# A vision tower with product-key feed-forward on one core: front attention moved seven slots, search tiles one, gathered rows weighted on ScalarE, look-ups in fours, head masks as a two-tensor product

## What is computed

```python
h = tok(x); h = concatenate([cls_tok, h], axis=1)          # 64 x 65 x 64
# attention, 8 heads of 8 channels, cosine form
qn, kn = q / max(norm(q), 1e-12), k / max(norm(k), 1e-12)
attn = softmax(einsum(qn, kn) * scale + bias[None])
h = h + (einsum(attn, v)) @ proj_w.T + proj_b              # input layernormed
# feed-forward: per token and head the 16 best of 64 x 64 product keys
scores, idx = top_k(sim, 16)                               # two sides, 64 keys each
score = scores[0][..., :, None] + scores[1][..., None, :]
final_scores, pk_idx = top_k(score, 16); w = softmax(final_scores)
k = einsum(w, keys_table[ind]); v = einsum(w, values_table[ind])
h = h + softmax(causal(q @ k)) @ v @ Wo                    # input layernormed
```

## Time and profile before

| | us |
|---|---|
| median of 3 runs | 3051.8 (3051.78 to 3052.03) |
| the profiled execution: its own time | 3053.45 |
| its span, first to last instruction | 3051.4 |
| mean granted TensorE clock | 0.998 |
| units of pass 0 (5 images) | 258.7 |
| units of passes 1 to 6 (7 images), each | 309.4 to 310.7 |
| units of pass 7 (7 images, front of 5) | 300.4 |
| units of pass 8 and 9 (5 images) | 251.4 and 225.8 |

### The profile page before, as it was taken

How to read it: one execution, slowest core, us unless ns; L and a number is a source line. 1 busy time by engine, 2 the same in 40 slices (tenths; PEclk the granted TensorE clock), 3 DMA queues, 4 the chain that set the end, 5 groups by cost and what they waited for, 6 DMA issues and landing times.

```text
span 3051.4 us, 60054 instructions
## 1 busy us (share of the span) xinstructions
PE 2907.5 (95%) x16560; PEld 1968.0 (64%) x16560; DVE 2554.1 (84%) x10286; ACT 1730.3 (57%) x4926; POOL 1569.5 (51%) x3406
## 2 busy tenths in 40 slices
PE   8999999999999999999999999999999999999998
PEld 7867656665666566656665666566656666776666
DVE  4677789988998899889988898889888987777776
ACT  4465565555555555556555655565556555655554
POOL 2234356655665566555655565556655654333331
PEclk9999999999999999999999999999999999999999
DMA  9213211121111211121112111211121111010100
GB/s 214 50 45 79 52 31 33 32 37 34 32 32 31 41 29 32 32 40 30 30 31 45 25 32 32 40 31 33 32 38 33 33 33 38 20 24 20 25 20 19
DMA packets 121289, 117.47 MB, mean 38 GB/s; under 512 B 61491, under 2 KB 109310, under 8 KB 120958
## 3 DMA queue, kind: packets, MB, share of 16 engines
q1 hardware_dynamic: 105525, 83.84, 12.9%
q0 software_dynamic: 14336, 29.39, 5.6%
q10 hardware_dynamic: 1096, 0.41, 0.1%
HBM read 66.36 MB, written 9.84 MB: 25 GB/s over the span
## 4 chain that ended last, share of the span: by engine, by line
PE 53%; DVE 23%; issue 9%; POOL 7%; ACT 7%; ACTq 0%; DMA 0%; DVEq 0%; POOLq 0%
PE ps L831 27%; PE ps L819 11%; DVE wts L1230 11%; ACT wts L1005 4%; DVE x_sum L1297 2%; PE ps L755 2%; DVE top L1214 2%; PE ps L724 2%; PE ps L772 1%; PE ps L706 1%; POOL stat L528 1%; PE ps L862 1%; DVE cand_rest L1216 1%; DVE rest L1196 1%; POOL stat L525 1%
## 5 line engine op out<-in xcount | busy, mean ns | idle before, releaser
L831 PE MATMUL ps<-wts,table 128*128 128x455 f32 (+2 forms) x5120 | 2006.0, 474 | 0.0
L1230 DVE SCALAR_TENSOR_TENSOR wts<-ps,wts 128x455 f32<-128x455 f32 (+2 forms) x2560 | 1349.9, 531 | 383.4 <-ACT wts L1005 372.6
L819 PE MATMUL ps<-st,spread 128*128 128x456 f32 (+2 forms) x2560 | 1237.4, 483 | 119.0 <-DVE wts L1230 110.1
L1005 ACT ACTIVATE wts<-ps 128x455 f32<-128x455 f32 (+2 forms) x2560 | 1126.6, 475 | 86.8 <-PE ps L819 78.5
L831 PEld LDWEIGHTS ps<-wts,table 128*128 128x128 f32 x5120 | 905.4, 190 | 104.1 <-issue 44.4
L819 PEld LDWEIGHTS ps<-st,spread 128*128 128x128 f32 x2560 | 482.2, 188 | 603.0 <-DVE wts L1230 524.3
L591 POOL DMA_INDIRECT x_rows<-folded,x_r x448 | 453.8, 1013 | 85.9 <-issue 80.9
L524 POOL TENSOR_SCALAR stat<-top 110x1 f32<-110x1 f32 (+1 forms) x268 | 70.7, 264 | 760.1 <-DVE top L1214 756.2
L511 POOL TENSOR_TENSOR cand<-best 110x15 f32<-110x15 f32 (+5 forms) x804 | 160.4, 226 | 221.0 <-DVE best L1198 219.5
L980 ACT ACTIVATE cand_e<-top,stat 110x16 f32<-110x16 f32 (+1 forms) x268 | 82.3, 307 | 297.1 <-POOL stat L531 296.3
L976 ACT ACTIVATE sc<-ps 110x128 f32<-110x128 f32 (+1 forms) x268 | 74.2, 277 | 255.9 <-PE ps L772 255.6
(11 more groups left out here) (186 smaller groups left out, 3762.3 us busy)
## 6 DMA issues: line engine op xcount, KB each, us to landing
st<-st SPq DMA_DIRECT2D x320, 114.0 KB, 2.3
table<-in_table SPq DMA_DIRECT2D x128, 128.0 KB, 5.0
rz_row<-rz_dram SPq DMA_DIRECT2D x52, 165.0 KB
folded<-table SPq DMA_DIRECT2D x64, 128.0 KB, 2.6
x_rows<-folded,x_r POOLq DMA_INDIRECT x448
rz_row<-rz_dram SPq DMA_DIRECT2D x28, 228.0 KB
scratch<-in_x SPq DMA_DIRECT2D x7, 343.0 KB, 4.5
rz_dram<-rz SPq DMA_DIRECT2D x52, 1.3 KB
```

Of the source, the lines that this page charges most:

```text
L819: mm(ps[0:128, g % NA, 0:t], spread[:, q * 128:(q + 1) * 128], st[:, k % 2, ORDER[c // QUADS], 0:t], start=True, stop=True).then_inc(a_rea ...
L831: mm(ps[0:128, ACC + k % 2, 0:t], table[:, k % H, i, :], wts[:, g % RING, 0:t], start=(c == 0), stop=(c == CH - 1)).then_inc(out_done, 1)
L1005: A(wts[:, g % RING, 0:t], ps[0:128, g % NA, 0:t], ACT.Exp).then_inc(e_ready, 1)
L1230: V.scalar_tensor_tensor(out=wts[:, g % RING, 0:t], in0=ps[0:128, g % NA, 0:t], scalar=0.0, in1=wts[:, g % RING, 0:t], op0=ALU.is_ge, op1= ...
```

## The change

It alters six things:

1. `ATT` goes from `LN1` + 28 to `LN1` + 35. With that the task steps fall on slots 1 (mask), 3 (scores), 4, 5, 6 (POOL), 8, 11, 12, 14 of a head and the same plus 16; the reciprocal and the scaling move to task steps 12 and 13.
2. Tiles and picks start 15 slots ahead instead of 16 (`LEAD`).
3. The gathered blocks are multiplied by their weights on ScalarE, one instruction each (16 per pick, every third slot from 29), and VectorE adds blocks of four (three adds of 512 columns), then halves (256 and 128 columns).
4. The 16 look-ups are done four at a time: compare, multiply and reduce over 4 x 69 = 276 elements, 12 instructions in slots 17 to 28.
5. The sum of a task's exponentials comes from TensorE: the values get a column of ones (9 columns per head instead of 8), and the reciprocal reads PSUM. The VectorE sum (L1153) goes.
6. `kx` is made by a tensor-tensor product on POOL, and the layernorm's root and reciprocal become a power of -0.5 on POOL (slot +6); ScalarE only adds epsilon there. Some buffers move into `scratch`; the second buffers of `expo` (passes 1 to 9) and `pt` go.

```diff
-SLOTS = 4
+BATCH = 4
+BATCHES = TOPK // BATCH
+GAP = 3
+ADDS = 5
+GROUP = (0, 1, 2, 1)
-TILE_START = {CH * (k - 1) - 16 + 8 * (t + sparse(k)): (k, t) for k in range(HEADS) for t in range(tiles(k))}
-PICK_START = {CH * (k - 1) - 16: j for j, k in enumerate(PICKS)}
+LEAD = 15
+TILE_START = {CH * (k - 1) - LEAD + 8 * (t + sparse(k)): (k, t) for k in range(HEADS) for t in range(tiles(k))}
+PICK_START = {CH * (k - 1) - LEAD: j for j, k in enumerate(PICKS)}
-QK, VAL, NRM, ATT = LN1 + 11, LN1 + 14, LN1 + 17, LN1 + 28
+QK, VAL, NRM, ATT = LN1 + 11, LN1 + 14, LN1 + 17, LN1 + 35
-X_NEG, X_WEIGHT, X_POS, X_ZINV, X_NORM, X_ROW, X_FOUND = 13, 14, 15, 16, 17, 17, 21
-X_GATHER, X_ADD, X_TURN, X_MOVE = 22, 30, 77, 78
+X_NEG, X_WEIGHT, X_POS, X_ZINV, X_NORM, X_ROW, X_FOUND = 13, 14, 15, 16, 17, 17, 20
+X_GATHER, X_SCALE, X_ADD, X_TURN, X_MOVE = 22, 29, 39, 78, 79
...
 POOL, layernorm and mask
+            def layernorm(p, q, n, start):
+                i = 2 * p + n
+                if q == start + 6:
+                    pool.wait_ge(std_ready, i + 1)
+                    P.tensor_tensor(std[:, 0:PASSES[p]], std[:, 0:PASSES[p]], power[:, 0:PASSES[p]], ALU.pow)\
+                        .then_inc(inv_ready, 1)
-                    P.tensor_scalar(kx[0:C, 0:t], xf[:, 0:t], head_of[0:C, j:j + 1], None, ALU.mult)\
+                    P.tensor_tensor(kx[0:C, 0:t], xf[:, 0:t], head_of[0:C, j:j + 1].to_broadcast([C, t]), ALU.mult)\
...
 POOL, gathers
-                        if r % 4 == 0:
-                            pool.wait_ge(x_found, 4 * j + r // 4 + 1)
+                        if r % BATCH == 0:
+                            pool.wait_ge(x_found, BATCHES * (j + 1) if b == 2 else BATCHES * j + b + 1)
+                            if b == 0 and j >= 1:
+                                pool.wait_ge(x_turned, j)
+                            if b == 3:
+                                pool.wait_ge(x_add, ADDS * j + 1)
-                        if TOPK * j + r >= SLOTS:
-                            pool.wait_ge(x_add, TOPK * j + r - SLOTS + 1)
...
 ScalarE
-                    A(std[:, 0:PASSES[p]], ps[0:L, FR, 0:PASSES[p]], ACT.Sqrt, bias=eps[0:L, 0:1])\
+                    A(std[:, 0:PASSES[p]], ps[0:L, FR, 0:PASSES[p]], ACT.Identity, bias=eps[0:L, 0:1])\
+                for r in range(TOPK):
+                    j = pick_at(g, X_SCALE + GAP * r)
+                    if j is not None:
+                        if r == 0:
+                            act.wait_ge(x_norm, j + 1)
+                        act.wait_ge(x_in[r % (2 * BATCH)], 16 * (TOPK // (2 * BATCH) * j + r // (2 * BATCH) + 1))
+                        row = x_rows[:, GROUP[r // BATCH], r % BATCH, :]
+                        A(row, row, ACT.Copy, scale=x_w[:, j % 2, r:r + 1]).then_inc(x_scaled, 1)
...
 VectorE, attention of the front
-                j = task_at(p, q, 6)
-                if j is not None:
-                    dve.wait_ge(s_exp, base + j + 1)
-                    if j >= 2:
-                        dve.wait_ge(o_out, base + j - 1)
-                    V.tensor_reduce(red[:, j % 2, 1, 0:n], by_image(expo[:, j % 2, 0:t], n), AX.X, ALU.add)\
-                        .then_inc(s_sum, 1)
+                j = task_at(p, q, 12)
...
+                    V.reciprocal(red[:, j % 2, 1, 0:n], ps[0:L, bank("output", p), HD:n * (HD + 1):HD + 1])\
+                        .then_inc(s_inv, 1)
...
 VectorE, picks
+                for b in range(1, BATCHES):
+                    j = pick_at(g, X_ADD + GAP * BATCH * b)
+                    if j is not None:
+                        dve.wait_ge(x_scaled, TOPK * j + BATCH * (b + 1))
+                        if b >= 2:
+                            dve.wait_ge(x_add, ADDS * j + b - 1)
+                        V.tensor_tensor(x_rows[:, 0, :, :], x_rows[:, 0, :, :], x_rows[:, GROUP[b], :, :], ALU.add)\
+                            .then_inc(x_add, 1)
+                for half in (2, 1):
+                    j = pick_at(g, X_TURN - half)
...
-                        V.scalar_tensor_tensor(out=x_sum[:, :], in0=iota[:, :], scalar=x_pf[:, r:r + 1], in1=x_at[:, :],
-                                               op0=ALU.is_equal, op1=ALU.mult, accum_out=x_rf[:, r:r + 1])\
-                            .then_inc(x_row, 1)
+                        shape = [128, BATCH, NCAND]
+                        if step % 3 == 0:
+                            V.tensor_tensor(x_hit[:, :, :], iota[:, :].unsqueeze(1).to_broadcast(shape),
+                                            x_pf[:, BATCH * b:BATCH * (b + 1)].unsqueeze(2).to_broadcast(shape),
+                                            ALU.is_equal).then_inc(x_row, 1)
+                        if step % 3 == 1:
+                            V.tensor_tensor(x_hit[:, :, :], x_hit[:, :, :], x_at[:, :].unsqueeze(1).to_broadcast(shape),
+                                            ALU.mult).then_inc(x_row, 1)
+                        if step % 3 == 2:
+                            V.tensor_reduce(x_rf[:, BATCH * b:BATCH * (b + 1)], x_hit[:, :, :], AX.X, ALU.add)\
+                                .then_inc(x_row, 1)
```

## The result

The changed kernel takes 3144.4 us (3143.9 to 3146.5, four runs) against 3051.9 us: a ratio of 1.0304, 95% interval 1.0292 to 1.0316. It is slower by 93 us, where I forecast faster by 52. The time lies outside my range.

A forecast was written before the change was run, and what follows sets the result against it. TensorE was taken as the floor, with VectorE's lateness 7% above it. 3053.45 - 33 - 18 - 25 + 7 + 14 + 3 = 3001 us for the profiled execution, 3000 for the median; 8-in-10 range 2940 to 3054.

The forecast's parts named there:

- The three terms for the order of slots: Tiles one slot later -25 us, tasks piling up in slots 4 to 8 +14, second layernorm losing overlap in the prelude +3.
- The other terms: Less VectorE backlog -33 us, layernorms' table loads gone -18, the power late in POOL's slot 6 +7.
- The tiles one slot later: ScalarE's threshold wait moves from slots 14 and 30 to 15 and 31, 0.5 us off each place: -25 us (0 to 37).
- The pile-up of slots 4 to 8: Later tasks put 3.9 us on POOL before ScalarE's slot 8; charged 0.4 us in each of 36: 14 us (0 to 43).
- My third rival: POOL's 3.9 us chain in slots 4 to 8 isn't hidden and costs 115 us over 36 heads: 3101 us, chance 0.09.
- ScalarE's weightings: 448 added on ScalarE at 0.31 us, some 139 us against 51 us of table loads removed; taken as covered, no charge.
- VectorE's load: VectorE loses 434 us of work and gains 222, net 212 us; its busy time was to be near 2340 us.
- What that is worth: Lighter VectorE removes half of its own backlog's late spreads, 4.7 us in each of 7 passes: 33 us (0 to 66).
- (c): 38 late spreads of pass 3, 9.5 us together, put down to VectorE's own backlog.
- Table loads -18, power +7: Layernorms' two ScalarE loads per front go, 18 us; POOL's power at slot 6 delays TensorE, 0.4 us for each of 18.
- Head mask: POOL's tensor-tensor form was to cost 0.94 us instead of 1.45: 28 us less POOL time, no term in the sum.
- The rival about POOL: Look-ups in slots 6 to 9 stretched by POOL's run, 168 us of VectorE, backlog stays: 3033 us, chance 0.14.

The follow-up runs named there:

- the last run: Changed kernel with tasks, tiles, weighting, adding, look-ups and head mask as before, tile's sum one slot later on ScalarE: 0.9694, 2966.8 us against 3060.6, fastest of all.

## Why the prediction was wrong, point by point

The three terms for the order of slots (-25, +14 and +3 us) come to -8 us. They measured +79 us with the new instructions and +111 us in the kernel before. That is the step that failed most. The other terms (-33, -18 and +7 us) come to -44 us and measured +14 (1.0047).

*The tiles one slot later: -25 us, measured 0 alone, and some 40 us lost with the new forms.* The step that failed is "I take 0.5 us off each". The wait for the threshold comes from the distance of one slot between POOL's chain and ScalarE's sum, and both moved. Pass 9 of the changed kernel shows it as the prediction asked: slot 14 went from 0.85 to 0.10 us, but slot 31 keeps 0.79 of the 0.86 that slot 30 had, and slot 7 (0.55) and slot 28 (0.28) are new; the head has its 29.1 us as before. I had named this wait, and priced moving both ends of it. Moving one end, as the last run does with the tiles at their old slots, is worth 59 us (0.0194 of 3060).

*The pile-up of slots 4 to 8: +14 us charged, the largest cost.* Both moves together cost the kernel before 111 us, and putting the tasks alone back in the changed kernel gives 39 us. My third rival had the place and the engines (POOL's run from the threshold to the second subtraction, ScalarE at slot 8) and 3101 us, at 9 in 100. The chance was far too small, for two reasons that the rows could have told me. First, I counted POOL's work of slot 6 and left out slot 22, where a gather of 1.07 us stands between the chain and the subtraction; slots 23 and 24 hold 7.2 us of pass 3. (The sign that I had named, ScalarE idle for over 2 us at slot 8, didn't show in that form: there it waits some 0.3 us for the subtraction, after 1.6 us at the median for the threshold at slot 7, and 1.5 us at most at slot 24.) Second, "ScalarE and TensorE have other work there" was no argument against: the other work of ScalarE stood *behind* the waiting instruction.

*ScalarE's weightings: nothing charged, 28 us.* "Under its 40% of slack" is the failed step. The duration was also taken too low (0.31 us, where 0.39 were measured). The idle time of an in-order engine covers only what doesn't stand ahead of a unit that the chain of spreads waits for.

*VectorE's load: near 2340 us expected, 2437 measured.* The new instructions cost nearly what I had worked out, 233 us against 222 (the groups by form, compare):

```profile
L1323 DVE TENSOR_TENSOR x_rows<-x_rows 128x512 f32<-128x512 f32 x84 | 59.0, 702 | 0.0
L1346 DVE TENSOR_TENSOR x_rows<-iota,x_pf 128x276 f32<-128x276 f32 x112 | 58.1, 519 | 0.0
L1350 DVE TENSOR_TENSOR x_rows<-x_rows,x_at 128x276 f32<-128x276 f32 x112 | 49.1, 438 | 0.0
L1353 DVE TENSOR_REDUCE x_rf<-x_rows 128x4 f32<-128x276 f32 x112 | 47.4, 423 | 0.0
L1330 DVE TENSOR_TENSOR x_rows<-x_rows 128x256 f32<-128x256 f32 x28 | 11.6, 413 | 0.0
L1330 DVE TENSOR_TENSOR x_rows<-x_rows 128x128 f32<-128x128 f32 x28 | 7.6, 272 | 0.0
```

The error is in what the removed ones gave back. By the timeline a VectorE instruction starts before the one ahead of it has ended, so durations overlap: over the whole run they sum to 3190.9 us before and to 2991.5 after, while busy time is 2554.1 and 2437.1. Of 199 us of durations only 117 are time; 968 instructions fewer have each given back 0.085 us less than their row says.

*What that is worth: 33 us.* The column of ones alone gave 26. Batches and adds by fours removed instructions too and gained nothing: the second put its work on ScalarE, and with the first ScalarE waits longer. So (c) was not mainly VectorE's load; the fastest kernel has VectorE at 84%, as before, and half the lateness.

*Table loads -18, power +7: -11 us together, measured -8 ± 6.* Right in sum, wrong in the parts: the power takes 1.52 us for 7 columns, just above my upper bound and not in the lower third, and TensorE waits 1.64 us for it in the pass above. The layernorms' table loads went, and with them the exponential's reloads (59 to 21, where I had 20).

*Head mask: 28 us of POOL for nothing.* Hidden, I said; the two-tensor form costs 14 us (0.45%), by a way that I hadn't in mind, the 14 look-ups that it holds up. The rival about POOL, that it holds the new VectorE instructions, decided little: of the 112 first instructions of a batch 34 were stretched, by 9.8 us in all, not 168.

## To carry to other kernels

When each engine takes its instructions in a fixed order, look for instructions that wait for another engine with critical work queued behind them, and try moving the waiting end later, not the work. Here one slot on ScalarE was worth 59 us in one kernel, more than any saved work, and 14 us in another where the slot behind was taken, so it has to be measured in place. A change of places has to be priced together with the other changes of places: 0.7% and 0.0% made 3.6%. Slack of an engine is no cover for an instruction that stands ahead of the critical one.

## What the hardware showed that I had not expected

A power of -0.5 on POOL took 1.52 us for 65 x 7 elements, as long as a product with a scalar over 65 times as many columns. ScalarE's copy with a scale per partition took 0.39 us for 128 x 128 out of SBUF. POOL's tensor-tensor over 64 x 455 elements held 14 VectorE look-ups, which have two SBUF inputs, until its own end (1.74 instead of 0.27 us), and the product with a scalar in its place only slowed 14 of them (0.28 to 0.43 us), so that 0.96 us on POOL can cost more than 1.46. Small tensor-tensors of POOL, 110 x 15 to 110 x 32 elements, left a look-up beside them at 0.28 us. The Trainium skill (SBUF — State Buffer, SBUF: two separate sides) says that whichever starts first gets the shared ports for its whole instruction and the other is blocked, when VectorE's instruction has two SBUF inputs and POOL's reads SBUF. The rows with the large tensor-tensor agree in that the look-up is held until POOL's end, though it is shown to start first; the 0.43 us beside the product with a scalar and the 0.28 us beside the small ones speak against it.

The changed kernel is granted half of TensorE's clock (1.2 instead of 2.4 GHz) in the first 4.7 us of its passes and then for 3.4 us once in each of passes 0 to 2 and 4 to 8; the kernel before, from the start of its passes to the end of the last product, only in the first 3.4 us. Two stretches of 3.4 us (columns as in the windows above):

```profile
799.60:803.00 3.40, 3.40 (x10) 1.89 (x8) 3.40 (x19) 1.01 (x3) 1.32 (x3) 0.51 0.00 0
1120.40:1123.80 3.40, 2.38 (x8) 1.34 (x9) 3.40 (x20) 1.68 (x6) 0.85 (x1) 1.00 0.02 5
```

The first is in pass 2, right behind the two table loads of the q and k norms, for which TensorE stood idle for 2.03 us; the second is the same place of pass 3, which kept its clock. Pass 2 takes 321.5 us and pass 3 322.7. So such a window costs nothing that shows in a pass, and the 93 us are not the clock's.
